# Where a Trainium2 kernel takes its norm roots, and in which order three engines meet between a gated layer and a linear attention

## The chip, the cores and the metric

One core of one Trainium2 chip. The metric is the time of the kernel on the device in microseconds, the median of several runs. Five engines of the core work side by side, each through its own list of instructions, and wait for each other on semaphores: TensorE (PE, with its weight loads as PEld), VectorE (DVE), ScalarE (ACT), GpSimd (POOL) and SyncE (SP), which issues the DMAs.

## What is computed

Four sequences (B = 4) of 512 rows by 256 columns, float32, go through four parts, with a residual and a normalisation over the columns after each:

```
x = layernorm(x + attention_0(x))      # softmax attention
x = layernorm(x + wave(x))             # gated layer, below
x = layernorm(x + attention_1(x))      # linear attention
x = layernorm(x + mlp(x))              # six blocks, 256 -> 1024 -> 256

wave: h = (cos(ph) + sin(ph)) * amp                # amp = sigmoid, ph = tanh of x @ weights
      for l in range(2):
          h = layernorm(h + (h @ ent_w[l]) @ ent_pw[l])
          h = layernorm(h + sum over two paths of h @ path_w[l] * mod[l])
attention_1: q = elu(x Wq)+1, k = elu(x Wk)+1, v = x Wv
      out = (q (k^T v)) / (q . sum(k)),  then @ Wo
```

The change touches the wave, attention_1 and the first turn of the MLP. What they compute stays the same.

## The kernel before

Every product is made from two parts of each float32 operand, a high part (rounded to the engine's format, ScalarE) and a low part (the remainder, VectorE), in three matmuls: high by high, high by low, low by high. So every tensor that goes into TensorE passes through ScalarE and then VectorE.

**The wave.** The two products of half a layer are folded into one 256x256 matrix, so the wave is four *stages* (STAGES = 4, END = 3) of one product and one normalisation for each of the four sequences b. One pass of one sequence is: `linear(st, b)` on TensorE into two PSUM banks (L1652, L1654); `moments(st, b)` on VectorE, that is mean and variance from PSUM (L2200, L2204); the *root*, one over the square root of the variance by an integer start value and two polynomial steps; `normalise(st, b)` on ScalarE (L1944), which needs the root's scale and shift; `turn` on TensorE, the transposes (L1661); `high` on ScalarE (L1951); `low` on VectorE (L2219); and then the next stage's `linear`. After the stages comes `sum_up(b)` on VectorE: the last gain, the residual (L2227, L2230), moments again; `output_of_wave(b)` on ScalarE (L1960) writes attention_1's input, `final_turn(b, c)` on TensorE (L1672) transposes it, `output_high` (L1955) and `output_low` (L2237) split it.

**Where a root is taken.** `ON_VECTOR` and `ON_GPSIMD` list the keys ("stage", st, b), ("sum", b) and ("next", b). For a key of `ON_GPSIMD`, VectorE's `statistics` stops after the moments and raises `v_mv`, and GpSimd's `root` takes 14 small dependent instructions (L135 to L146, L1604, L1606) and raises `g_scale`. For a key of `ON_VECTOR`, VectorE itself goes on with 9 steps (L96 to L121) and one for the shift (L2192), and raises `v_scale`. GpSimd takes its roots one by one in the order of the list.

**Attention_1.** For each b six *units* (`unit(b, at)`: four of keys and values, two of queries; TensorE L1699, ScalarE L1972, L1973, L1979, VectorE L2252), then `key_values` (L1713), `block_diagonal` (L2262), `numerators` in two halves (L1728), `divide` (L2271, L2273, L2278), `transpose_attention` (L1741), `attention_high` and `attention_low` (L1988, L2287), `project` (L1750), `residual_next` (L2294), `moments_next`, a root with the key ("next", b), `normalise_next` (L1997), `transpose_next` (L1762) and the halves `next_high` and `next_low` (L2003, L2303). TensorE may start unit n when ScalarE has done unit n - 3. Behind it come the MLP's `hidden` (L1808), `gelu` (L2049, L2050) and `gelu_low` (L2326), and `output` (L1825).

**What sets the order.** The order on each engine is written out by hand, as a list of such calls; an engine that waits holds up everything behind it in its own list. Two waits outside these lists matter here. SyncE loads the MLP's rows over the memory of the wave's sums once the last `output_of_wave` is done:

```
sp.wait_ge(wave["a_norm"], number("sum", B - 1))
for tile, name in ((g.mlp_b2, ...), (g.mlp_g, ...), (g.mlp_b, ...)):
    sp.dma_start(tile, ...).then_inc(rows_in, 16)
```

and GpSimd waits for these rows before the first root of a "next" key, since it adds them right behind (L1616 to x_a, L1621 to mlp_b):

```
pool.wait_ge(rows_in, 16 * 4)
for b in range(B):
    if b < B - 1:
        root("next", b)
```

## Time and profile before

| What | us |
|---|---|
| median of 3 runs (1121.85 to 1127.71) | 1122.81 |
| the profiled execution: its own time | 1125.32 |
| the profiled execution: span of the trace | 1123.6 |
| TensorE busy | 1020.4 (91%) |
| VectorE busy | 749.5 (67%) |
| ScalarE busy | 621.6 (55%) |
| GpSimd busy | 355.9 (32%) |
| chain that ended last: PE, DVE, ACT, POOL | 71%, 13%, 6%, 4% |

Attention_0 and the start of the wave's gates take the first 353 us of the span, the wave's stages run to about 441, attention_1 with the first pieces of the MLP to 563, and the MLP to the end. The share of an engine is an average over all of these; what a change in one stretch is worth has to be read in that stretch.

### The profile page before, as it was taken

The page shows a single profiled execution, that of the slowest core. Times are in us where ns is not written, and L with a number is a line of the kernel's source. Part 1 is how long each engine was busy: PE and PEld are TensorE (multiplying, and loading weights), DVE is VectorE, ACT ScalarE, POOL GpSimd, SP SyncE. Part 2 cuts the span into 40 slices and gives each one's busy share as a digit, 9 for nine tenths or more (in the row PEclk, how much of TensorE's full clock was granted, in tenths as well). Part 3 has the DMA queues.
Part 4 walks back from the last instruction along what each step waited for, and adds up shares of the span by engine and source line. Part 5 has one row for each costly group of instructions (what it writes and reads, how often), then busy time and mean ns, then how long its engine had stood idle before and what let it go on. Part 6 is the DMA issues. An engine that isn't in the chain of part 4 may idle for free.

```text
span 1123.6 us, 18216 instructions
## 1 busy us (share of the span) xinstructions
PE 1020.4 (91%) x6589; PEld 847.2 (75%) x6589; DVE 749.5 (67%) x2023; ACT 621.6 (55%) x1200; POOL 355.9 (32%) x704
## 2 busy tenths in 40 slices
PE   6788998989988787878799999999999999999996
PEld 5455555555656686666698999988999899998896
DVE  4676775867628567757656776666776777666756
ACT  4466565664358455645565664566645666456650
POOL 3454354461122555413201224212232122321500
PEclk9599988998989899789999999999999999999998
DMA  7000000022110001011110110101011011010111
GB/s 234 20 2 20 2 20 20 21 58 76 57 43 3 1 1 38 1 75 57 39 57 1 38 31 9 38 1 38 2 38 38 1 38 38 1 38 1 38 39 38
DMA packets 29234, 36.91 MB, mean 33 GB/s; under 512 B 1780, under 2 KB 26584, under 8 KB 29144
## 3 DMA queue, kind: packets, MB, share of 16 engines
q1 hardware_dynamic: 24600, 31.02, 8.5%
q10 hardware_dynamic: 4544, 4.72, 1.4%
q8 instruction: 53, 0.87, 0.3%
q14 instruction: 37, 0.30, 0.1%
HBM read 31.40 MB, written 4.20 MB: 32 GB/s over the span
## 4 chain that ended last, share of the span: by engine, by line
PE 71%; DVE 13%; ACT 6%; issue 4%; POOL 4%; DMA 1%; SPq 0%; DVEq 0%; ACTq 0%; POOLq 0%
PE ps L1825 23%; PE ps L1808 23%; PE ps L853 3%; PE ps L806 3%; PE ps L830 3%; DVE ps L1065 3%; PE ps L901 2%; PE ps L1781 2%; PE ps L860 2%; PE ps L1351 1%; PE ps L817 1%; DVE ln_stats L2200 1%; PE ps L1699 1%; PE ps L1652 1%; PE ps L869 1%
## 5 line engine op out<-in xcount | busy, mean ns | idle before, releaser
L2049 ACT ACTIVATE G<-ps,bias_col 128x512 f32<-128x512 f32 x192 | 135.4, 705 | 181.3 <-PE ps L1808 171.8
L1825 PE MATMUL ps<-w_h,G_h 128*128 128x256 f32 x736 | 208.2, 283 | 0.0
L1825 PE MATMUL ps<-w_h,G_l 128*128 128x256 f32 x736 | 207.9, 282 | 0.0
L1825 PE MATMUL ps<-w_l,G_h 128*128 128x256 f32 x736 | 207.8, 282 | 0.0
L2326 DVE TENSOR_TENSOR G_l<-G,G_h 128x512 fp32r<-128x512 f32 x192 | 155.1, 816 | 63.3 <-ACT G_h L2050 63.2
L1628 POOL TENSOR_TENSOR x_a<-xn,mlp_g 128x1024 f32<-128x1024 f32 x20 | 67.6, 3378 | 350.1 <-DVE xn L2356 350.1
L681 ACT ACTIVATE probs<-ps 128x512 f32<-128x512 f32 (+3 forms) x256 | 98.3, 440 | 113.1 <-PE ps L817 112.9
L1808 PE MATMUL ps<-xT_h,w_h 128*128 128x512 f32 x384 | 152.0, 396 | 1.6 <-ACT G_h L2050 1.6
L1065 DVE CUSTOM_DVE_ANT_0 ps<-ps,q_mask 128x128 f32<-128x128 f32 (+3 forms) x256 | 120.7, 512 | 46.8 <-PE ps L806 45.3
L1808 PE MATMUL ps<-xT_h,w_l 128*128 128x512 f32 x384 | 150.6, 392 | 0.0
L1808 PE MATMUL ps<-xT_l,w_h 128*128 128x512 f32 x384 | 150.3, 391 | 0.0
L1825 PEld LDWEIGHTS ps<-w_h,G_h 128*128 128x128 f32 x736 | 139.9, 190 | 0.7
L1825 PEld LDWEIGHTS ps<-w_h,G_l 128*128 128x128 f32 x736 | 140.3, 191 | 0.0
L1825 PEld LDWEIGHTS ps<-w_l,G_h 128*128 128x128 f32 x736 | 139.5, 190 | 0.8
L2050 ACT ACTIVATE G_h<-ps,bias_col 128x512 fp32r<-128x512 f32 x192 | 134.9, 703 | 0.0
L2340 DVE TENSOR_TENSOR rsum<-ps,x_a 128x1024 f32<-128x1024 f32 x23 | 28.2, 1225 | 105.2 <-PE ps L1825 105.2
L569 POOL TENSOR_SCALAR_AFFINE_SELECT probs<-probs 128x256 f32<-128x256 f32 x128 | 53.1, 416 | 123.4 <-ACT probs L681 123.4
L1808 PEld LDWEIGHTS ps<-xT_h,w_h 128*128 128x128 f32 x384 | 72.1, 188 | 16.8 <-ACT G_h L2050 2.1
L1808 PEld LDWEIGHTS ps<-xT_h,w_l 128*128 128x128 f32 x384 | 72.1, 188 | 15.6
L1808 PEld LDWEIGHTS ps<-xT_l,w_h 128*128 128x128 f32 x384 | 72.2, 188 | 15.0
L806 PE MATMUL ps<-heads_T 64*128 64x128 f32 (+3 forms) x256 | 73.2, 450 | 10.8 <-DVE top_score L1065 9.7
L2320 DVE TENSOR_TENSOR xT_l<-hs,xT_h 128x512 fp32r<-128x512 f32 x40 | 77.0, 1952 | 2.3 <-ACT xT_h L2035 1.1
(298 smaller groups left out, 2142.4 us busy)
## 6 DMA issues: line engine op xcount, KB each, us to landing
w_raw<-L_ffn_W_T SPq DMA_DIRECT2D x12, 1024.0 KB, 5.1
hs<-L_attn_hidden_states SPq DMA_DIRECT2D x8, 512.0 KB, 4.0
...
heads_T<-neg_rows SPq DMA_DIRECT2D x64, 2.0 KB
```

Source lines behind the costliest of these rows:

```text
L569: pool.affine_select(diagonal, diagonal, [[0, 2], [1, P]], ALU.is_ge, 0.0, base=0, channel_multiplier=-1).then_inc(s["g_sel"], 1)
L681: act.activation(probs[:, p % 2, o, OFF[j]:OFF[j] + COLS[j]], ps[:, score_bank(r, o), 0:COLS[j]], ACT.Exp).then_inc(s["a_exp"], 1)
L806: pe.matmul(ps[:, o, 0:(t + 1) * P], heads_T[rows, p // UP, 0, p % UP, t * P:(t + 1) * P], heads_T[rows, p // UP, 1, p % UP, 0:(t + 1) * P ...
L830: mm = pe.matmul(outputs[rows:rows + 2 * DH, j * P:S], val[:, j, 4 * q + h, :], probs[:, h // 2, h % 2, OFF[j]:OFF[j] + COLS[j]], start=(r ...
L1065: v.tensor_tensor_reduce(ps[:, o, 0:(t + 1) * P], ps[:, o, 0:(t + 1) * P], q_mask[:, S - (t + 1) * P:S], 1.0, MASKED, ALU.add, ALU.max, to ...
L1628: pool.tensor_tensor(g.x_a[:, rows, :], xn[:, b % 2, :, :], bcast(g.mlp_g[:, i, :], 1, [P, RT, D]), ALU.mult).then_inc(feed["g_mul"], 1)
L1808: mm = pe.matmul(ps[:, hidden_bank(i, n), :], w[:, c, f * P:(f + 1) * P], x[:, b, c, :], start=(k == 0), stop=(k == 5))
L1825: mm = pe.matmul(ps[:, 4 + t // 2, (t % 2) * D:(t % 2 + 1) * D], x[b % 2][f][:, t * P:(t + 1) * P], w2_chunk(w, f), start=(k == 0), stop=( ...
L2049: act.activation(G32[n % 4], bank, ACT.Gelu, bias=bias)
L2050: act.activation(G_h[b % 2][f], bank, ACT.Gelu, bias=bias).then_inc(feed["a_g"], 1)
L2320: v.tensor_tensor(g.xT_l[:, b, c, :], src, g.xT_h[:, b, c, :].bitcast(F32), ALU.subtract).then_inc(feed["v_T"], 1)
L2326: v.tensor_tensor(G_l[b % 2][f], G32[n % 4], G_h[b % 2][f].bitcast(F32), ALU.subtract).then_inc(feed["v_gl"], 1)
```

## The change

1. Three roots go from GpSimd to VectorE: ("stage", 0, 0), ("stage", END, 0) and ("next", 2). `moments` becomes a generator, and `gated_low(2)` is put between the moments and the steps of the first of these roots.
2. On ScalarE at the wave's begin, `gated_high(2)` goes ahead of the sines of b = 3, and `normalise(0, 2)` goes behind `high(0, 0)`.
3. At the wave's end, VectorE's first two instructions of `sum_up(0)` go ahead of the last `low`, and the rest right behind it.
4. In attention_1, `block_diagonal(0)` goes ahead of the end of `sum_up(2)`, whose statistics go behind `unit(1, 0)`; `divide(0, 1)` goes ahead of the start of `sum_up(3)`; the two final turns of b = 3 go behind unit(2, 2) and unit(2, 4) (TensorE, and their halves on ScalarE and VectorE); `output_of_wave(3)` on ScalarE goes behind unit(2, 0).
5. At the MLP's begin, the first two `hidden` go ahead of `key_values(3)` and of the second `transpose_next` of b = 1, with a wait of `hidden` for its own bank alone, and `gelu`, `gelu_low`, `attention_high(3)` and `attention_low(3)` are moved to fit.

```diff
...
     NORMS = [("stage", st, b) for st in range(STAGES) for b in range(B) if (st, b) < (END, 2)]
     NORMS += [("sum", 0), ("stage", END, 2), ("sum", 1), ("stage", END, 3), ("sum", 2), ("sum", 3)]
     NORMS += [("next", b) for b in range(B)]
-    ON_VECTOR = [("sum", 0), ("sum", 1), ("next", B - 1)]
-    ON_GPSIMD = [("stage", st, b) for st in range(STAGES) for b in range(B)]
-    ON_GPSIMD += [("sum", 2), ("sum", 3), *(("next", b) for b in range(B - 1))]
+    ON_VECTOR = [("stage", 0, 0), ("stage", END, 0), ("sum", 0), ("sum", 1), ("next", 2), ("next", 3)]
+    ON_GPSIMD = [key for key in NORMS if key not in ON_VECTOR]
...
-        for key in ON_GPSIMD[:1 - B]:
-            root(*key)
+        for key in ON_GPSIMD:
+            if key[0] != "next":
+                root(*key)
         pool.wait_ge(rows_in, 16 * 4)
         for b in range(B):
-            if b < B - 1:
+            if ("next", b) in ON_GPSIMD:
                 root("next", b)
...
                 if b == 0 and f % 2 == 0 and not early:
                     pe.wait_ge(feed["v_w"], i * 8 - 4 + f // 2 + 1)
                 if early and n < 3:
-                    pe.wait_ge(second["a_exp"], B * UNITS)
+
+                    pe.wait_ge(second["a_exp"], B * UNITS - 2 + n)
                     pe.wait_ge(second["a_v"], B * RT)
                 elif early and n in (*range(3, FC), FC + 1, FC + 2):
                     pe.wait_ge(feed["a_g"], n - 2)
...
         unit(1, 5)
         key_values(1)
         project(0)
-        final_turn(3, 0)
         numerators(1, 0)
         unit(2, 0)
-        final_turn(3, 1)
         numerators(1, 1)
         unit(2, 1)
         transpose_attention(1)
-        for at in range(2, UNITS):
-            unit(2, at)
+        unit(2, 2)
+        final_turn(3, 0)
+        unit(2, 3)
+        unit(2, 4)
+        final_turn(3, 1)
+        unit(2, 5)
         key_values(2)
         project(1)
         transpose_next(0, 0)
...
         transpose_attention(2)
         for at in range(2, UNITS):
             unit(3, at)
+        hidden(0, 0, (0,))
         key_values(3)
         project(2)
         transpose_next(1, 0)
         numerators(3, 0)
+        hidden(0, 0, (1,))
         transpose_next(1, 1)
-        hidden(0, 0, (0, 1))
         numerators(3, 1)
         hidden(0, 0, (2, 3))
         transpose_attention(3)
...
         gated_high(act, g, 1)
         for n in range(4 * (B - 1), 4 * B):
             gate_function(act, g, n)
+        gated_high(act, g, 2)
         half_angle(act, g, 3)
-        gated_high(act, g, 2)
         whole_angle(act, g, 3)
         normalise(0, 0)
         gated_high(act, g, 3)
         normalise(0, 1)
-        normalise(0, 2)
         for st in range(END):
 
             for b in range(B):
                 high(st, b)
-                if (st, b) != (0, 0):
-                    normalise(*divmod(st * B + b + 2, B))
+                normalise(*divmod(st * B + b + 2, B))
...
         output_high(2, 1)
         unit(1, 4)
         unit(1, 5)
+        unit(2, 0)
         output_of_wave(3)
-        output_high(3, 0)
-        unit(2, 0)
-        output_high(3, 1)
         unit(2, 1)
         attention_high(1)
         unit(2, 2)
+        output_high(3, 0)
+        unit(2, 3)
         normalise_next(0)
-        for at in range(3, UNITS):
-            unit(2, at)
+        unit(2, 4)
+        output_high(3, 1)
+        unit(2, 5)
...
         normalise_next(1)
         for at in range(3, UNITS):
             unit(3, at)
+        gelu(0, 0, 0)
         next_high(1, 0)
+        gelu(0, 0, 1)
         next_high(1, 1)
-        gelu(0, 0, 0)
-        gelu(0, 0, 1)
         normalise_next(2)
         gelu(0, 0, 2)
+        attention_high(3)
         gelu(0, 0, 3)
-        attention_high(3)
         gelu(0, 0, 4)
         gelu(0, 0, 5)
         next_high(2, 0)
...
             if st + b == 0:
 
                 v.wait_ge(first["g_x1"], B + 1)
-            for _ in statistics(banks(b), ("stage", st, b)):
-                pass
+            yield from statistics(banks(b), ("stage", st, b))
 
         def low(st, b):
             for c in range(KC):
...
                 low_next(i, 0)
 
 
+        def run(steps, count=100):
+            for _ in range(count):
+                next(steps, None)
+
         square(v, g, chain, 1)
         gated_low(v, g, 0)
         gated(v, g, chain, 1)
         square(v, g, chain, 2)
         gated_low(v, g, 1)
         gated(v, g, chain, 2)
-        moments(0, 0)
+        steps = moments(0, 0)
+        run(steps, 2)
         gated_low(v, g, 2)
+        run(steps)
         square(v, g, chain, 3)
         gated(v, g, chain, 3)
-        moments(0, 1)
+        run(moments(0, 1))
         gated_low(v, g, 3)
-        moments(0, 2)
+        run(moments(0, 2))
         for st in range(END):
             if st == 1:
                 v.wait_ge(wave["a_l1"], 3)
...
             for b, (later, done) in TURN:
-                low(st, b)
-                if (st, b) != (END - 1, B - 1):
-                    moments(st + later, done)
-
-        def run(steps, count=100):
-            for _ in range(count):
-                next(steps, None)
-
-        run(sum_up(0))
-        moments(END, 2)
+                if (st, b) == (END - 1, B - 1):
+
+                    steps = sum_up(0)
+                    run(steps, 2)
+                    low(st, b)
+                    run(steps)
+                    run(moments(END, 2))
+                else:
+                    low(st, b)
+                    run(moments(st + later, done))
+
         steps = sum_up(1)
         run(steps, 1)
         for c in range(KC):
...
         unit(0, 1)
         run(steps)
         unit(0, 2)
-        moments(END, 3)
+        run(moments(END, 3))
         unit(0, 3)
         steps = sum_up(2)
         run(steps, 1)
...
         for c in range(KC):
             output_low(1, c)
         unit(0, 5)
+        block_diagonal(0)
+        run(steps, 1)
+        unit(1, 0)
         run(steps)
-        block_diagonal(0)
-        unit(1, 0)
         divide(0, 0)
         unit(1, 1)
+        divide(0, 1)
         steps = sum_up(3)
         run(steps, 1)
-        divide(0, 1)
         unit(1, 2)
         output_low(2, 0)
         unit(1, 3)
...
         run(steps)
         unit(1, 5)
         block_diagonal(1)
-        output_low(3, 0)
+        residual_next(0)
         divide(1, 0)
         unit(2, 0)
-        residual_next(0)
-        output_low(3, 1)
         run(moments_next(0))
         divide(1, 1)
         unit(2, 1)
         attention_low(1)
-        for at in range(2, UNITS):
-            unit(2, at)
+        unit(2, 2)
+        output_low(3, 0)
+        unit(2, 3)
+        output_low(3, 1)
+        unit(2, 4)
+        unit(2, 5)
...
         for at in range(2, UNITS):
             unit(3, at)
         block_diagonal(3)
+        gelu_low(0, 0, 0)
         residual_next(2)
         next_low(1, 0)
         divide(3, 0)
         run(moments_next(2))
+        gelu_low(0, 0, 1)
         next_low(1, 1)
-        gelu_low(0, 0, 0)
         divide(3, 1)
-        gelu_low(0, 0, 1)
         gelu_low(0, 0, 2)
+        attention_low(3)
         gelu_low(0, 0, 3)
-        attention_low(3)
         gelu_low(0, 0, 4)
         gelu_low(0, 0, 5)
         residual_next(3)
```

**The first place is VectorE at the wave's begin**, from the last gate of b = 2 on (`amp` is what the gate gives, `x_b` its work tile, L1396 is `gated_low`). Before:

```order
L1385 SCALAR_TENSOR_TENSOR amp<-x_b,amp 128x1024
L2200 BN_STATS ln_stats<-ps 128x6 x4
L2204 BN_AGGR norm_mv<-ln_stats 128x2 x4
L1396 TENSOR_TENSOR xT_l<-amp,xT_h 128x1024
L1375 SCALAR_TENSOR_TENSOR x_b<-x_b 128x1024
```

and now:

```order
L1385 SCALAR_TENSOR_TENSOR amp<-x_b,amp 128x1024
L86 BN_STATS ln_stats<-ps 128x6 x4
L91 BN_AGGR ln_mv<-ln_stats 128x2 x4
L1396 TENSOR_TENSOR xT_l<-amp,xT_h 128x1024
L96 TENSOR_SCALAR ln_var<-ln_mv 128x4
L99 TENSOR_SCALAR norm_factors<-ln_var 128x4
L103 TENSOR_TENSOR ln_t<-norm_factors 128x4
...
L121 SCALAR_TENSOR_TENSOR norm_factors<-ln_t,norm_factors 128x4
L2195 SCALAR_TENSOR_TENSOR norm_factors<-ln_mv,norm_factors 128x4
L1375 SCALAR_TENSOR_TENSOR x_b<-x_b 128x1024
```

The root's ten small instructions stand between `gated_low(2)` and the square of b = 3.

On ScalarE at the same place, before and then now (L1365 and L1370 are the sines of b = 3, L1391 `gated_high`, L1944 and L1948 `normalise`, L1951 and L1955 `high`):

```order
L1365 ACT_TABLE_LOAD
L1365 ACTIVATE x_b<-tanh 128x1024
L1391 ACTIVATE xT_h<-amp 128x1024
L1370 ACTIVATE tanh<-tanh 128x1024
L1944 ACTIVATE xn<-ps,norm_shift,norm_scale 128x256 x4
L1391 ACTIVATE xT_h<-amp 128x1024
L1944 ACTIVATE xn<-ps,norm_shift,norm_scale 128x256 x4
L1944 ACTIVATE hs<-ps,norm_shift,norm_scale 128x256 x4
L1951 ACTIVATE xT_h<-ps 128x512 x4
```

```order
L1391 ACTIVATE xT_h<-amp 128x1024
L1365 ACT_TABLE_LOAD
L1365 ACTIVATE x_b<-tanh 128x1024
L1370 ACTIVATE tanh<-tanh 128x1024
L1948 ACTIVATE xn<-ps,norm_factors 128x256 x4
L1391 ACTIVATE xT_h<-amp 128x1024
L1948 ACTIVATE xn<-ps,norm_shift,norm_scale 128x256 x4
L1955 ACTIVATE xT_h<-ps 128x512 x2
L1948 ACTIVATE hs<-ps,norm_shift,norm_scale 128x256 x4
```

The first `high` no longer stands behind the third `normalise`.

**The second place is VectorE at the wave's end** (L2227 and L2229 are the first instruction of `sum_up`, the last L2219 or L2221 is the last `low`). Before:

```order
L2204 BN_AGGR norm_mv<-ln_stats 128x2 x4
L2219 TENSOR_TENSOR xT_l<-ps,xT_h 128x512 x2
L2227 TENSOR_TENSOR amp<-xn,last_g 128x1024
L2230 TENSOR_TENSOR amp<-amp,x_a 128x1024
L86 BN_STATS ln_stats<-amp 128x6 x4
```

and now:

```order
L2207 BN_AGGR norm_mv<-ln_stats 128x2 x4
L2229 TENSOR_TENSOR amp<-xn,last_g 128x1024
L2232 TENSOR_TENSOR amp<-amp,x_a 128x1024
L2221 TENSOR_TENSOR xT_l<-ps,xT_h 128x512 x2
L86 BN_STATS ln_stats<-amp 128x6 x4
```

The sum's two long instructions stand ahead of the last low part.

**The third place is VectorE around the third of the residuals of attention_1** (rsum; G_l_0 and G_l_1 are the low parts of the first two gelu tiles, z and att the divisions of b = 3). Before:

```order
L2294 TENSOR_TENSOR rsum<-ps,x_b 128x1024
L2303 TENSOR_TENSOR xT_l<-ps,xT_h 128x512
L2271 TENSOR_SCALAR z<-ps 128x32
L2273 RECIPROCAL z<-z 128x32
L2278 TENSOR_TENSOR att_5532<-ps,z 128x256 x2
L2200 BN_STATS ln_stats<-rsum 128x6 x4
L2204 BN_AGGR norm_mv<-ln_stats 128x2 x4
L2303 TENSOR_TENSOR xT_l<-ps,xT_h 128x512
L2326 TENSOR_TENSOR G_l_0_5560<-G_0_5576,G_h_0_5544 128x512
L2271 TENSOR_SCALAR z<-ps 128x32
```

and now:

```order
L2328 TENSOR_TENSOR G_l_0_5560<-G_0_5576,G_h_0_5544 128x512
L2296 TENSOR_TENSOR rsum<-ps,x_b 128x1024
L2305 TENSOR_TENSOR xT_l<-ps,xT_h 128x512
...
L86 BN_STATS ln_stats<-rsum 128x6 x4
L91 BN_AGGR ln_mv<-ln_stats 128x2 x4
L96 TENSOR_SCALAR ln_var<-ln_mv 128x4
...
L2195 SCALAR_TENSOR_TENSOR norm_factors<-ln_mv,norm_factors 128x4
L2328 TENSOR_TENSOR G_l_1_5561<-G_1_5577,G_h_1_5545 128x512
L2305 TENSOR_TENSOR xT_l<-ps,xT_h 128x512
L2273 TENSOR_SCALAR z<-ps 128x32
```

The steps of the root now stand ahead of the second division of b = 3.

## Rows read from the trace of the kernel before

**Rows 1.** Busy time by stretch; PE, PEld, DVE, ACT, POOL busy, then granted clock, DMA share, GB/s.
```profile
353.00:383.00 30.00, 18.17 (x131) 16.72 (x129) 19.02 (x37) 18.48 (x27) 13.31 (x43) 0.93 0.01 3
...
563.00:1100.00 537.00, 537.00 (x3491) 490.56 (x3490) 367.63 (x777) 308.77 (x504) 134.36 (x45) 1.00 0.08 25
```
**Rows 2.** Timeline, ScalarE, wave's begin; start, us, engine, line, operation [idle before <-releaser].
```profile
370.32 1.94 ACT L1944 ACTIVATE xn<-ps,norm_shift,norm_scale 128x256 f32<-128x256 f32 x4 [5.29 <-POOL norm_shift L1606]
...
375.73 1.94 ACT L1944 ACTIVATE xn<-ps,norm_shift,norm_scale 128x256 f32<-128x256 f32 x4 [2.53 <-POOL norm_shift L1606]
...
382.15 2.07 ACT L1951 ACTIVATE xT_h<-ps 128x512 fp32r<-128x512 f32 x4
```
**Rows 3.** Timeline, first and last of the 14 instructions of one GpSimd root.
```profile
418.25 0.19 POOL L135 TENSOR_SCALAR norm_var<-norm_mv 128x4 f32<-128x4 f32 x1 [0.60 <-POOL norm_shift L1606]
...
421.94 0.23 POOL L1606 TENSOR_SCALAR norm_shift<-norm_shift 128x4 f32<-128x4 f32 x1
```
**Rows 4.** Timeline, VectorE, the wave's last two passes and the first sum.
```profile
434.87 1.29 DVE L2219 TENSOR_TENSOR xT_l<-ps,xT_h 128x512 fp32r<-128x512 f32 x2 [1.59 <-ACT xT_h L1951]
436.08 1.41 DVE L2200 BATCH_NORM_STATS2 ln_stats<-ps 128x6 f32<-128x256 f32 x4
...
439.83 1.29 DVE L2219 TENSOR_TENSOR xT_l<-ps,xT_h 128x512 fp32r<-128x512 f32 x2 [1.92 <-ACT xT_h L1951]
441.04 1.21 DVE L2227 TENSOR_TENSOR amp<-xn,last_g 128x1024 f32<-128x1024 f32 x1
...
445.40 0.17 DVE L96 TENSOR_SCALAR ln_var<-ln_mv 128x4 f32<-128x4 f32 x1
...
447.18 0.16 DVE L2192 SCALAR_TENSOR_TENSOR norm_factors<-ln_mv,norm_factors 128x4 f32<-128x4 f32 x1
```
**Rows 5.** Timeline, ScalarE, the first output of the wave.
```profile
447.38 2.07 ACT L1960 ACTIVATE x_b<-amp,norm_factors 128x256 f32<-128x256 f32 x4 [1.52 <-DVE norm_factors L2192]
```
**Rows 6.** Timeline, VectorE's third gated low part.
```profile
364.11 1.23 DVE L1396 TENSOR_TENSOR xT_l<-amp,xT_h 128x1024 fp32r<-128x1024 f32 x1 [1.69 <-ACT xT_h L1391]
```
**Rows 7.** Timeline, GpSimd in the same microsecond, in the root of ("stage", 0, 0).
```profile
364.20 1.20 POOL L141 TENSOR_TENSOR norm_t<-norm_scale 128x4 f32<-128x4 f32 x1
```
**Rows 8.** Busy time of PE by stretch, with the granted clock, ahead of the first final turn.
```profile
446.00:448.00 2.00, 0.00 (x0) 0.84 0.00 0
```
**Rows 9.** Timeline, ScalarE, the last stage's normalise of b = 3.
```profile
469.41 1.94 ACT L1944 ACTIVATE hs<-ps,norm_shift,norm_scale 128x256 f32<-128x256 f32 x4 [2.90 <-POOL norm_shift L1606]
```
**Rows 10.** Timeline, VectorE, unit(1, 0).
```profile
471.93 0.42 DVE L2252 SCALAR_TENSOR_TENSOR k<-ex,pos 128x256 f32<-128x256 f32 x1 [1.14 <-ACT pos L1973]
```
**Rows 11.** Timeline, GpSimd's start on the roots of ("sum", 2) and ("next", 0), then mlp_b.
```profile
470.54 0.19 POOL L135 TENSOR_SCALAR norm_var<-norm_mv 128x4 f32<-128x4 f32 x1 [1.17 <-issue]
...
503.66 0.20 POOL L135 TENSOR_SCALAR norm_var<-norm_mv 128x4 f32<-128x4 f32 x1 [12.38 <-DVE norm_mv L2204]
...
514.08 3.11 POOL L1621 TENSOR_TENSOR mlp_b<-mlp_b,mlp_b 128x1280 f32<-128x1280 f32 x1
```
**Rows 12.** Timeline, ScalarE, output_of_wave(3) and normalise_next(0).
```profile
491.31 2.07 ACT L1960 ACTIVATE x_b<-amp,norm_shift,norm_scale 128x256 f32<-128x256 f32 x4 [6.04 <-POOL norm_shift L1606]
...
509.53 2.08 ACT L1997 ACTIVATE hs<-rsum,norm_shift,norm_scale 128x256 f32<-128x256 f32 x4
```
**Rows 13.** The last of the rows' DMAs: its issue by SyncE.
```profile
494.26 0.43 SPq L1543 DMA_DIRECT2D mlp_b<-L_ffn_LN_B  x1
```
**Rows 14.** The same DMA: size and median us from issue to landing.
```profile
mlp_b<-L_ffn_LN_B SPq DMA_DIRECT2D x1, 640.0 KB, 6.1
```
**Rows 15.** Timeline, TensorE, the first numerators of b = 2.
```profile
521.08 1.19 PE L1728 MATMUL ps<-bd,q 128*128 128x136 f32 x8 [1.38 <-DVE bd L2263]
```
**Rows 16.** Timeline, VectorE, the moments of ("next", 2).
```profile
544.99 1.39 DVE L2200 BATCH_NORM_STATS2 ln_stats<-rsum 128x6 f32<-128x256 f32 x4
```
**Rows 17.** Timeline, ScalarE, normalise_next(2).
```profile
551.65 2.08 ACT L1997 ACTIVATE hs<-rsum,norm_shift,norm_scale 128x256 f32<-128x256 f32 x4 [2.69 <-POOL norm_shift L1606]
```
**Rows 18.** The chain that ended last, in order of time: the last projection.
```profile
558.65 4.38 PE ps L1750 x24
```

## Prediction

> **What bounds the kernel now.** I read the busy time by stretch first, to see where the end can be moved. From 563 us on TensorE is busy for all 537 of 537 us at full clock, while between 353 and 383 it is busy for 18.2 of 30 [rows 1]. So before 563 the kernel waits, behind it the MLP takes what it takes, and a microsecond won in front of 563 moves the end by a microsecond. Then I read the timelines of the four engines from 353 to 563 side by side, with the waits in brackets, and asked at each idle stretch of TensorE which call came last. Three places answer for what the change touches.
>
> At the wave's begin ScalarE waits 5.29 us for the first root and 2.53 for the second, and reaches the first `high` at 382.15, behind three normalises [rows 2]. In the stages a pass is a loop of two slots: normalise 1.94 [rows 2], half a `high` (0.5), `low` 1.29 and moments 1.8 [rows 4], a GpSimd root from 418.25 to 422.17, that is 3.92 [rows 3], some 0.1 between each. Together 9.7 for two passes; the last two `low` are 4.96 apart [rows 4]. At the end `output_of_wave(0)` starts at 447.38 and frees TensorE at 449.45 [rows 5]. In attention_1 TensorE waits for `output_of_wave(3)`, which itself waited 6.04 for its root [rows 12], and later for VectorE.
>
> The numbers below are replays: I take each engine's new list, give every call its duration from the rows, and start it at the latest of its waits and the end of the call ahead of it. All times are in the clock of the old trace.
>
> **The wave's begin.** `gated_high(2)` now comes right after the gates, so `gated_low(2)` runs in the gap behind the moments instead of waiting 1.69 until 364.11 [rows 6], and ends about 363.6. The ten small steps take 1.94, from 445.40 to 447.34 where VectorE does them today [rows 4], so the first scale is there at 365.6 and `normalise(0, 0)` starts then and not at 370.32 [rows 2]: 4.7 earlier. It doesn't help by itself. The second root still runs on GpSimd, and its moments are pushed behind the ten steps: they end at about 371.0 against 370.8. `normalise(0, 1)` starts near 376.0 instead of 375.73 [rows 2]. What counts is that the first `high` comes next, at 377.9 and not 382.15 [rows 2]. That is **4.3 us**.
>
> A port matters here. GpSimd's instruction at 364.20 took 1.20 [rows 7] where its like take 0.2, and ended with VectorE's 1024-column low part (364.11 to 365.34) [rows 6]. `gated_low(3)` now starts with the second root and costs it 1.0, which is in the sum. The Trainium skill (SBUF — State Buffer, "Who interferes with whom") states that VectorE with two SBUF inputs and GpSimd hold a shared port in turn, and whoever starts first keeps it for its whole instruction. By that rule the second root could lose 0 instead of 1.0 if GpSimd starts first; the rows here show the loss, the trace agrees with the lock, and the sum keeps 1.0.
>
> **The stages.** The loop is the same, so the 4.3 is carried, with one more saving. ("stage", END, 0) costs 1.94 on VectorE in place of 3.92 on GpSimd: 2.0. But ScalarE is then still in the normalise ahead of it and has a `high` to do first, so about 1.1 of it comes through for `normalise(END, 0)`, and the ten steps delay VectorE's next `low` little, which had 1.59 of slack [rows 4]. Also the second `high` ran right behind the first one and found its inputs late; now the even passes are up to 6 us earlier than before and the odd ones 4.5 to 5. The replay has `normalise(END, 0)` end at 432.5 (old 439.3) and the last moments of stage END, b = 1, end at 433.1.
>
> **The wave's end.** `sum_up(0)` waited for the last `low` until 441.04 [rows 4]. Now it starts at 433.1, its two long instructions (1.21 and 1.23) end at 435.6, and the last `low` follows, ending at 436.8, 4.3 ahead of the old 441.12. Statistics 1.8 and ten steps 1.94 end at 440.6. GpSimd's root of (END, 1) meets the long instructions as it does today and ends near 439.1, `normalise(END, 1)` takes ScalarE until 441.1, and then `output_of_wave(0)` goes at 441.1 instead of 447.38 [rows 5]. So the wave is **6.3 us** earlier. Bounds: 4.3, if nothing is won in or behind the stages, and 8.3, if the clock stays up as well. The clock: in 446 to 448, with TensorE idle, the granted clock is 0.84 of full, so it fell to 1.2 GHz at about 447.4 [rows 8], some 2.5 after the last product; the replay's new idle is 2.6. I count nothing for it and keep 2 us for the upper end.
>
> **Attention_1, middle.** Here is the trap. Measured in a clock shifted by the 6.3, `block_diagonal(0)` no longer waits behind sum 2, which frees the first numerators by 2.5. But sum 2's statistics now stand behind unit(1, 0), which waits for ScalarE's normalise of 469.41 [rows 9] and runs at 471.93 to 472.35 [rows 10]. With 1.8 of statistics GpSimd starts that root at 474.2, not 470.54 [rows 11]; its output leaves ScalarE 2.4 later, and so does what follows, up to project(0), ending at 491.1. There the moved final turn pays: numerators(1, 0) and unit(2, 0) no longer wait for `output_of_wave(3)`, and run 3 to 4 us earlier than before. But ScalarE now does unit(2, 0) first, so `output_of_wave(3)` ends near 496.6 and not 493.38 [rows 12]. The MLP's rows follow it: the last is issued at 494.26 [rows 13] and lands 6.1 later [rows 14], 7.0 behind the output. That is 503.6 now. GpSimd sits on this wait ahead of the root of ("next", 0), whose moments are ready at 496.5. So the root runs from 503.7, the same time as today's 503.66 [rows 11], and of the 5 to 6 us that TensorE had won almost all is given back. Only ScalarE is now free when the root is done: `normalise_next(0)` goes at 507.7 instead of 509.53 [rows 12]. The addition to mlp_b (3.11) [rows 11] blocks VectorE's queries as before, and the numerators of b = 2, at 521.08 today [rows 15], go at 519.3 to 519.6. **1.5 us**. TensorE idles some 7 us ahead of them; the products behind run at half clock, but VectorE's divisions are later than they. Bounds: -2 (the half clock and the later root both show) and +5 (the rows land in time).
>
> **The MLP's begin.** The first `hidden` fits into TensorE's wait ahead of key_values(3), and the second into the one ahead of the transposes, so numerators(3, 1) comes 1.7 earlier. The root of ("next", 2): moments start at 544.99 [rows 16], 1.8 and 1.94 later the factors are there, at 548.8, and `normalise_next(2)` starts at 548.85 instead of 551.65 [rows 17]: 2.8 earlier. VectorE pays with 1.94 ahead of the second division, which ends at 551.5 rather than 549.8, and the attention's transposes end at 552.5, 0.6 late. But the third gelu is done at 552.1 and `attention_high(3)` follows it directly. GpSimd's addition (551.1 to 553.5) holds one low part, then comes `attention_low(3)`, and the last project starts at 555.5 instead of 558.65 [rows 18]. **3.1 us**; its 4.38 [rows 18] is a run at half clock, and at full clock it would be 1.4 less. Bounds: 0.6 (VectorE's longer list cancels the root) and 4.5.
>
> **Sum.** 6.3 + 1.5 + 3.1 = 10.9. Against the profiled execution's 1125.32 that is 1114.4. The median of the three runs is 2.5 below that execution, at 1122.81; 10.9 below it is **1111.9**, my forecast. A measurement of this kernel tells about 0.5%, or 5.6 us, from no change.
>
> **The rivals.** (A) *The clock stays up* in the idle of the first final turn and at the last project: 2 and 1.4 more, 1108.5. For it: both idles shrink to about the length at which it fell. Against: rows of exactly that length show it falling. 0.22. (B) *The middle loses*: sum 2's late root and the late rows are dearer than I think, -2 instead of +1.5, and the tail gives 2: 6.3 - 2 + 2 = 6.3, 1116.5. For it: every wait there is on the edge and TensorE goes cold. 0.2. (C) *No change to be told*: the second root bounds the wave's begin, a cold TensorE in the first stages eats 2 of the 4.3, the middle gives -1 and the tail 0.6: 4.3 - 2 + 1 of the wave's end, -1, +0.6, so 2.9, 1119.9. 0.1. (D) *Slower*: `output_of_wave(3)` decides. Each microsecond by which it slips delays the rows, GpSimd's root, `normalise_next(0)` with units (2, 4) and (2, 5) queued behind it, and the numerators of b = 2. It loses from the point at which it ends 10.9 later than my 496.6, which eats the whole sum, that is when as much as another root (3.9) and another landing (7.0) come in between; at 15 later the kernel takes 1122.8 + 4.1 = 1126.9. The rows show GpSimd idle there, so 0.03. That the change doesn't do what it says is no case: the new lists are fixed.
>
> **How the numbers follow.** Forecast 0.45, A 0.22, B 0.2, C 0.1, D 0.03. The forecast's own range is 1109.5 to 1114.5. The range for eight in ten takes in A and most of B: 1107 to 1118. Faster by over 0.5% (below 1117.2) are the forecast, A and most of B: 0.85; same 0.12; slower 0.03.
>
> **What would show it.** First `high` about 4 us earlier on ScalarE, with one GpSimd root between it and normalise(0, 0); first final turn at 443; GpSimd's root of ("next", 0) starting with the landing of mlp_b, with a wait of some 7 us ahead of it, and TensorE idle ahead of numerators(2, 0); the last project at about 547.7. I am wrong if that root starts with its moments, if the first final turn is not 5 us or more earlier, or if the MLP from its first full turn on takes longer than today.

## The result, and the profile after

| | before | after |
|---|---|---|
| median, 4 runs of each | 1122.33 us (1115.84 to 1127.71) | **1107.94 us** (1106.56 to 1111.8) |
| profiled execution, own time | 1125.32 | 1107.9 |
| its span | 1123.6 | 1106.2 |

The ratio of the runs is estimated at 0.9884 with a 95% interval of 0.9836 to 0.9932: 1.16% or 13.0 us faster, where 10.9 were forecast; the two medians are 14.4 apart. The time is inside the range, 4.0 us below the forecast. Of those 4, 0.5 is the level of the runs: the forecast started from 1122.81.

The page of the changed kernel gives the shares. 13 us are hardly seen in them, since they were idle time.

```profile
span 1106.2 us, 18200 instructions
...
PE 1013.3 (92%) x6589; PEld 841.9 (76%) x6589; DVE 752.4 (68%) x2053; ACT 620.3 (56%) x1200; POOL 342.6 (31%) x662
```

**A marker for reading the two traces.** The spans differ by 17.4 us, which is more than the medians do. Where does that come from? I take as zero the start of the last gate instruction of b = 2 on VectorE (L1385), the last one whose predecessors the change leaves alone, and call it M. M is at 359.46 before and at 355.51 after. So 3.95 of the 17.4 lie in front of everything that was changed, and 13.4 behind it. All times "from M" below are free of the first part.

| us from M: start of | before | before, again | after | after, again |
|---|---|---|---|---|
| M itself, in the span | 359.46 | 357.09 | 355.51 | 356.89 |
| `normalise(0, 0)` | 10.9 | 10.9 | 6.0 | 6.0 |
| first `high` | 22.7 | 22.6 | 18.2 | 18.1 |
| `output_of_wave(0)` | 87.9 | 88.2 | 81.2 | 81.2 |
| `output_of_wave(1)` | 101.2 | 101.5 | 94.5 | 92.6 |
| `output_of_wave(3)` | 131.9 | 131.8 | 128.2 | 126.3 |
| GpSimd's root of ("next", 0) | 144.2 | 144.3 | 137.3 | 135.4 |
| `normalise_next(0)` | 150.1 | 149.4 | 141.3 | 139.3 |
| numerators(2, 0) | 161.6 | 161.0 | 152.4 | 150.5 |
| last `project` | 199.2 | 200.2 | 187.3 | 185.4 |
| end of the span | 764.1 | 765.2 | 750.7 | 748.7 |

**The wave's begin.** ScalarE's timeline after (start, us, engine, line, operation, idle before). `normalise(0, 0)` goes at 361.50 and the second root's wait is now the one of 5.57 us, in front of 371.85. The `high` at 373.66 follows at once, where before a third normalise lay between [rows 2].

```profile
361.50 1.93 ACT L1948 ACTIVATE xn<-ps,norm_factors 128x256 f32<-128x256 f32 x4 [0.20 <-DVE norm_factors L2195]
365.22 1.06 ACT L1391 ACTIVATE xT_h<-amp 128x1024 fp32r<-128x1024 f32 x1 [1.80 <-DVE amp L1385]
...
371.85 1.93 ACT L1948 ACTIVATE xn<-ps,norm_shift,norm_scale 128x256 f32<-128x256 f32 x4 [5.57 <-POOL norm_shift L1605]
373.66 1.09 ACT L1955 ACTIVATE xT_h<-ps 128x512 fp32r<-128x512 f32 x2
```

**The wave's end.** VectorE after: the two long instructions of the sum stand ahead of the last `low` and not behind it [rows 4].

```profile
428.89 1.19 DVE L2229 TENSOR_TENSOR amp<-xn,last_g 128x1024 f32<-128x1024 f32 x1
430.12 1.23 DVE L2232 TENSOR_TENSOR amp<-amp,x_a 128x1024 f32<-128x1024 f32 x1
431.26 1.28 DVE L2221 TENSOR_TENSOR xT_l<-ps,xT_h 128x512 fp32r<-128x512 f32 x2
...
434.31 0.17 DVE L96 TENSOR_SCALAR ln_var<-ln_mv 128x4 f32<-128x4 f32 x1
...
436.09 0.16 DVE L2195 SCALAR_TENSOR_TENSOR norm_factors<-ln_mv,norm_factors 128x4 f32<-128x4 f32 x1
```

ScalarE after (L1964 is `output_of_wave`, L2001 `normalise_next`). `output_of_wave(0)` at 436.69 has no wait any more [rows 5]: ScalarE itself is late, since the normalise ahead of it waited 5.91 for GpSimd. Below, `output_of_wave(3)` at 483.73 has no wait either, and `normalise_next(0)` and `normalise_next(2)` follow.

```profile
434.88 1.93 ACT L1948 ACTIVATE xn<-ps,norm_shift,norm_scale 128x256 f32<-128x256 f32 x4 [5.91 <-POOL norm_shift L1605]
436.69 2.08 ACT L1964 ACTIVATE x_b<-amp,norm_factors 128x256 f32<-128x256 f32 x4
...
483.73 2.07 ACT L1964 ACTIVATE x_b<-amp,norm_shift,norm_scale 128x256 f32<-128x256 f32 x4
...
496.78 2.08 ACT L2001 ACTIVATE hs<-rsum,norm_shift,norm_scale 128x256 f32<-128x256 f32 x4 [4.40 <-POOL norm_shift L1605]
...
536.49 2.07 ACT L2001 ACTIVATE hs<-rsum,norm_factors 128x256 f32<-128x256 f32 x4 [2.61 <-DVE norm_factors L2195]
```

**The middle.** GpSimd after: the root of ("next", 0) waits 9.71 us for a DMA, that of `mlp_b`, and not for its moments as before [rows 11]. `output_of_wave(3)` ended at 483.73 + 2.07 = 485.80, and the root starts 7.05 behind it. Of the 9.71, 2.75 would be there without the DMA (run 4). Then comes the addition to mlp_b.

```profile
492.85 0.19 POOL L135 TENSOR_SCALAR norm_var<-norm_mv 128x4 f32<-128x4 f32 x1 [9.71 <-DMA mlp_b<-L_ffn_LN_B]
...
499.00 2.35 POOL L1616 TENSOR_TENSOR x_a<-hs,mlp_b 128x1024 f32<-128x1024 f32 x1 [2.26 <-ACT hs L2001]
501.30 3.34 POOL L1621 TENSOR_TENSOR mlp_b<-mlp_b,mlp_b 128x1280 f32<-128x1280 f32 x1
```

The same DMA stands in the chain that ended last, after (start, us, what). Of it read how the chain goes from ScalarE's output into a DMA queue and back to a normalise, with TensorE nowhere in those 13 us. The last line is the last projection, 4.38 before [rows 18].

```profile
483.85 1.95 ACT x_b L1964 x4
486.20 0.43 SPq L1542
486.68 6.03 DMA mlp_b<-L_ffn_LN_B
...
497.28 1.57 ACT hs L2001 x3
...
542.85 3.00 PE ps L1750 x24
```

VectorE in the same place, then TensorE. The two `q` took 4.25 together beside GpSimd's 3.34 us instruction (one alone takes 0.68 or 0.69 elsewhere, and in the trace before one took 3.41 beside the same addition, of 3.11 there), and TensorE idled 6.13 ahead of numerators(2, 0), where it idled 1.38 before [rows 15].

```profile
500.33 0.69 DVE L2239 TENSOR_TENSOR xT_l<-ps,xT_h 128x512 fp32r<-128x512 f32 x1 [7.77 <-ACT xT_h L1959]
500.94 4.25 DVE L2254 SCALAR_TENSOR_TENSOR q<-ex,pos 128x512 f32<-128x512 f32 x2
505.11 2.35 DVE L2503 TENSOR_TENSOR w_l<-w_raw,w_h 128x1024 fp32r<-128x1024 f32 x2
```

```profile
507.93 1.50 PE L1728 MATMUL ps<-bd,q 128*128 128x136 f32 x5 [6.13 <-DVE bd L2265]
```

### The profile page after: what moved, and what is told of

It reads as the page before. It is cut to its first block, busy times and chain, and to the rows that moved or that the text cites. A ratio compares the mean times of both kernels' runs of the same rounds, so it can differ in the third digit from the quotient of the medians.

```text
span 1106.2 us, 18200 instructions
## 1 busy us (share of the span) xinstructions
PE 1013.3 (92%) x6589; PEld 841.9 (76%) x6589; DVE 752.4 (68%) x2053; ACT 620.3 (56%) x1200; POOL 342.6 (31%) x662
## 4 chain that ended last, share of the span: by engine, by line
PE 51%; DVE 3%; ACT 1%; issue 1%; DMA 1%; POOL 0%; SPq 0%; DVEq 0%; ACTq 0%; POOLq 0%
PE ps L1826 24%; PE ps L1809 23%; PE ps L1781 2%; PE ps L1699 1%; DMA mlp_b<-L_ffn_LN_B 1%; PE ps L1750 1%; DVE ln_stats L86 0%; PE ps L1728 0%; ACT x_b L1964 0%; ACT hs L2001 0%; PE ps L1741 0%; DVE q L2254 0%; DVE w_l L2503 0%; DVE k L2254 0%; ACT pos L1977 0%
## 5 line engine op out<-in xcount | busy, mean ns | idle before, releaser
L1628 POOL TENSOR_TENSOR x_a<-xn,mlp_g 128x1024 f32<-128x1024 f32 x20 | 67.6, 3378 | 350.1 <-DVE xn L2358 350.1
```

The source lines that it names most:

```text
L1628: pool.tensor_tensor(g.x_a[:, rows, :], xn[:, b % 2, :, :], bcast(g.mlp_g[:, i, :], 1, [P, RT, D]), ALU.mult).then_inc(feed["g_mul"], 1)
```

## Experiments

Each kernel is the changed one with the edit shown, but for the first. A time without "median" is of one execution. Beside the first eight, kernels before ran at a median of 1120.8 (7 runs); beside the last four, on another chip, at 1125.05 (11 runs).

**1. The kernel before, once more.** No edit.

> The kernel before, unchanged, for a second trace of it. Times are read from M, the start of the last gate instruction of b = 2 on VectorE (359.46 us in the first trace of before, 355.51 in that of after); nothing ahead of M is changed. Theory 1, the 3.95 us between the two M is scatter from one execution to the next: M lies anywhere within some us of these two, while the distances from M repeat within 0.5: first high at M + 22.7, output_of_wave(0) at M + 87.9, numerators(2, 0) at M + 161.6, last project at M + 199.2, end of the span at M + 764. Theory 2, the change itself moves M: M is 359.5 again within 0.5.

1123.98 us. From M it repeats the first profile within 0.7 us up to numerators(2, 0) and within 1.1 behind them (table above), where 0.5 was expected. M itself moved by 2.4. So stretches behind M can be compared to about 1 us from single profiles, and whole times can't.

**2. ScalarE's old order at the wave's begin.**

```diff
-        gated_high(act, g, 2)
         half_angle(act, g, 3)
+        gated_high(act, g, 2)
...
         normalise(0, 1)
+        normalise(0, 2)
...
-                normalise(*divmod(st * B + b + 2, B))
+                if (st, b) != (0, 0):
+                    normalise(*divmod(st * B + b + 2, B))
```

> After, with ScalarE's order at the wave's begin as before (high(0, 0) behind the third normalise, gated_high(2) behind the first sine), and the root of (stage, 0, 0) still on VectorE. Theory 1, ScalarE's order brings the begin: the first high waits for the third root and normalise, so it starts at about M + 22 instead of M + 18.2, and output_of_wave(0) at about M + 85, 4 us later than in after. Theory 2, the root on VectorE brings it: the first high stays within 1 us of M + 18.2.

1114.23 us. ScalarE of this kernel: the first normalise still has its factors from VectorE, but three normalises stand ahead of the first `high`.

```profile
362.37 1.93 ACT L1948 ACTIVATE xn<-ps,norm_factors 128x256 f32<-128x256 f32 x4 [2.21 <-DVE norm_factors L2197]
...
376.73 1.94 ACT L1948 ACTIVATE hs<-ps,norm_shift,norm_scale 128x256 f32<-128x256 f32 x4 [2.06 <-POOL norm_shift L1605]
378.55 2.07 ACT L1955 ACTIVATE xT_h<-ps 128x512 fp32r<-128x512 f32 x4
```

The first `high` is at 378.55 - 354.59 (its M) = 24.0 from M, later than in the kernel before (22.7), and `output_of_wave(0)` at 88.2, the old place, where 85 was expected. **Without the order on ScalarE the whole gain of the wave is gone.** The roots on VectorE and the earlier sum are worth nothing there by themselves. The two moves were taken back together, and no run has the new order alone with everything else old.

**3. Root ("stage", 0, 0) back on GpSimd**, its key taken out of `ON_VECTOR`.

```diff
-    ON_VECTOR = [("stage", 0, 0), ("stage", END, 0), ("sum", 0), ("sum", 1), ("next", 2), ("next", 3)]
+    ON_VECTOR = [("stage", END, 0), ("sum", 0), ("sum", 1), ("next", 2), ("next", 3)]
```

> After, with the root of (stage, 0, 0) on GpSimd again and all else as in after, ScalarE's new order too. Theory 1, this root gives nothing by itself, since the second one on GpSimd decides: the first root ends about 4.5 us later than in after, but the first high starts at M + 18.2 to M + 18.8 and output_of_wave(0) within 0.7 us of M + 81.2. Theory 2, it is needed: the second root now queues behind the first on GpSimd (a contended one takes 7.8 us) and the first high is 2 us or more late.

1109.26 us. ScalarE of this kernel:

```profile
367.20 1.93 ACT L1948 ACTIVATE xn<-ps,norm_shift,norm_scale 128x256 f32<-128x256 f32 x4 [5.16 <-POOL norm_shift L1605]
372.02 1.93 ACT L1948 ACTIVATE xn<-ps,norm_shift,norm_scale 128x256 f32<-128x256 f32 x4 [1.94 <-POOL norm_shift L1605]
373.83 1.09 ACT L1955 ACTIVATE xT_h<-ps 128x512 fp32r<-128x512 f32 x2
```

`normalise(0, 0)` is 4.9 later (10.9 from M), yet the first `high` is 0.6 *earlier* (17.6), and `output_of_wave(0)` at 81.4 is the same as with the change (81.2). A root that comes 4.9 us sooner is worth nothing, because the next root gates the first `high`.

**4. GpSimd's wait for the MLP's rows behind the root of ("next", 0).**

```diff
-        pool.wait_ge(rows_in, 16 * 4)
         for b in range(B):
             if ("next", b) in ON_GPSIMD:
                 root("next", b)
+            if b == 0:
+                pool.wait_ge(rows_in, 16 * 4)
```

> After, with GpSimd's wait for the MLP's rows moved behind the root of (next, 0); the rows are only read by the additions behind it. Theory 1, that wait gives back what the moved final turns win: the root starts with its moments, some 7 us earlier than in after, normalise_next(0) some 4 us earlier (M + 137 instead of M + 141.3), numerators(2, 0) 3 to 4.4 us earlier than M + 152.4, and the kernel is 3 to 4 us faster than after. Theory 2, the additions on GpSimd and VectorE's queue behind them set the place: normalise_next(0) is earlier, but numerators(2, 0) within 1 us of M + 152.4, and so is the end.

Median 1105.88 us (4 runs), ratio to before 0.9881 (0.9815 to 0.9947), which times alone can't tell from the change's. GpSimd of this kernel:

```profile
486.38 0.19 POOL L135 TENSOR_SCALAR norm_var<-norm_mv 128x4 f32<-128x4 f32 x1 [2.75 <-issue]
...
494.99 2.38 POOL L1617 TENSOR_TENSOR x_a<-hs,mlp_b 128x1024 f32<-128x1024 f32 x1 [4.51 <-ACT hs L2002]
```

The root starts 2.75 us behind what GpSimd did last, and not 9.71. numerators(2, 0) come at 149.1 from M (152.4 with the change), the end at 746.6 (750.7). `output_of_wave(1)` is itself 0.6 later here (95.1), and from there numerators(2, 0) take 54.0 and not 57.9. So the rows did hold the middle, at a price of 3.9. The addition of `mlp_b`, 3.41 here, still costs VectorE its time.

**5. Root ("stage", END, 0) back on GpSimd**, by the same kind of edit.

```diff
-    ON_VECTOR = [("stage", 0, 0), ("stage", END, 0), ("sum", 0), ("sum", 1), ("next", 2), ("next", 3)]
+    ON_VECTOR = [("stage", 0, 0), ("sum", 0), ("sum", 1), ("next", 2), ("next", 3)]
```

> After, with the root of (stage, END, 0) on GpSimd again. Theory 1 (the replay), about half of the 2.0 us that it saves comes through: the GpSimd root would end 2 us later than VectorE's steps did, the sum starts 1.2 later, and output_of_wave(0) goes at M + 82 to M + 82.5 instead of M + 81.2; the end moves by the same 0.8 to 1.2. Theory 2, VectorE's ten steps cost its own queue as much as the root gains: output_of_wave(0) within 0.3 of M + 81.2.

1107.69 us. `output_of_wave(0)` at 82.2 from M, 1.0 later, and it waits for its root again:

```profile
436.76 2.07 ACT L1964 ACTIVATE x_b<-amp,norm_factors 128x256 f32<-128x256 f32 x4 [1.17 <-DVE norm_factors L2195]
```

The place alone would show nothing, since runs 4, 8 and 11, which have this part of the changed kernel as it is, stand at 82.3 to 82.4. But those are late already at the last normalise ahead of stage END (68.5 to 68.6 from M, 67.7 with the change), and this run isn't (67.6). From that normalise to `output_of_wave(0)` it takes 14.6 here and 13.5 to 13.8 in the five others read. So this root is worth 0.8 to 1.1, and the wave keeps 5.6 or more of its 6.7 without it. The end is at 751.4, 0.7 later.

**6. Root ("next", 2) back on GpSimd**, the same way.

```diff
-    ON_VECTOR = [("stage", 0, 0), ("stage", END, 0), ("sum", 0), ("sum", 1), ("next", 2), ("next", 3)]
+    ON_VECTOR = [("stage", 0, 0), ("stage", END, 0), ("sum", 0), ("sum", 1), ("next", 3)]
```

> After, with the root of (next, 2) on GpSimd again and the new order around it kept. Theory 1, this root is most of the 2.7 us won between the numerators of b = 2 and the last project: normalise_next(2) starts 2.4 later (M + 183.4 instead of M + 181.0), the last project 1.5 to 2 later (M + 189.1 instead of M + 187.3), and if TensorE's clock falls in the longer idle, the end is 3 us or more later. Theory 2, the order of hidden, gelu and attention_high(3) won it: the last project stays within 0.7 of M + 187.3.

1111.97 us. From numerators(2, 0) to the last project it takes 190.4 - 153.1 = 37.3; with the change 34.9; before 37.6. The root is nearly the whole gain there, 2.4 of 2.7. The new order around it does bring numerators(3, 1) forward, with the root on GpSimd too (24.9 behind numerators(2, 0), 26.1 before), but little of it reaches the last project. From the last project to the end it takes 563.4, as with the change (also 563.4) and not as before (764.1 - 199.2 = 564.9): the project ran at full clock here too, though TensorE idled ahead of it. TensorE of this kernel:

```profile
543.66 0.50 PE L1809 MATMUL ps<-xT_h,w_h 128*128 128x512 f32 x1 [2.68 <-ACT G_h L2054]
```

**7. The first sum behind the last `low` again.**

```diff
-                    steps = sum_up(0)
-                    run(steps, 2)
                     low(st, b)
-                    run(steps)
+                    run(sum_up(0))
```

> After, with the last low ahead of the whole of sum_up(0) again. Theory 1, from the trace of after: VectorE is free at M + 73.4, both the sum's input (M + 72.5) and the last high (M + 73.5) are there, so the two orders fill the same stretch and output_of_wave(0) stays within 0.4 of M + 81.2; this part of the change gives nothing. Theory 2, the sum must go first: output_of_wave(0) 1.2 us or more later.

1116.67 us, which is misleading: M is at 363.1 and not 355.5. From M, `output_of_wave(0)` is 0.3 later and the end 1.1, about the scatter of run 1. The earlier sum gives at most 0.3 at its own place. The 7.6 us of M come from unchanged code; see the last section.

**8. Part 4 of the change undone** on TensorE, ScalarE and VectorE: the final turns of b = 3 ahead of the numerators of b = 1, `output_of_wave(3)` ahead of unit(2, 0), sum 2 ahead of `block_diagonal(0)`. TensorE's part:

```diff
         project(0)
+        final_turn(3, 0)
         numerators(1, 0)
         unit(2, 0)
+        final_turn(3, 1)
         numerators(1, 1)
...
-        unit(2, 2)
-        final_turn(3, 0)
-        unit(2, 3)
-        unit(2, 4)
-        final_turn(3, 1)
-        unit(2, 5)
+        for at in range(2, UNITS):
+            unit(2, at)
```

> After, with the whole middle of attention_1 (block_diagonal(0), the sums 2 and 3, output_of_wave(3) and the two final turns of b = 3) in the order of before. Theory 1, the middle won 1.5 to 2.5 us: output_of_wave(0) at M + 81.2, output_of_wave(3) at M + 125 instead of M + 128.2, numerators(2, 0) at M + 154 to M + 155 instead of M + 152.4, and the end 1.5 to 2.5 later. Theory 2, since the rows come 3 us earlier in this order, the middle gave nothing: numerators(2, 0) within 0.7 of M + 152.4.

1110.45 us. From `output_of_wave(1)` to numerators(2, 0) it takes 60.4, as before (60.4), against 57.9 with the change. The end is at 753.0, 2.3 later from M, but `output_of_wave(1)` is 0.6 later here already; from there to the end it takes 657.9 against 656.2. Part 4 is worth 2.5 at numerators(2, 0) and 1.7 at the end.

**9. The change, once more**, beside the next three. No edit.

> The changed kernel once more, for its time beside the kernel before and the next two on one chip, and for a second trace. Both theories expect the distances of its first trace from M (the start of the last gate instruction of b = 2) within 0.7 us: output_of_wave(0) M + 81.2, numerators(2, 0) M + 152.4 to M + 153.1, last project M + 187.3 to M + 188, end M + 750.7 to M + 751.4; M itself anywhere from 354 to 363; the time 12 to 14 us below the kernel before.

Median 1112.01 us (6 runs, 1106.6 to 1117.71) against 1125.05 (11 runs): ratio 0.9891 (0.9851 to 0.9932), again 13.0 us. The distances from M were expected within 0.7 and are, up to `output_of_wave(0)`; from `output_of_wave(1)` on all is 1.9 earlier. In this profile the first final turn ran at full clock. TensorE by stretch (busy, granted clock, DMA share, GB/s) and its first final turn, first in the changed kernel's first profile, then in this one:

```profile
436.00:438.00 2.00, 0.16 (x2) 1.00 0.00 0
438.00:440.00 2.00, 1.18 (x6) 0.72 0.00 0
440.00:442.00 2.00, 0.79 (x4) 0.50 0.00 0
...
438.82 1.97 PE L1672 MATMUL ps<-ident,x_b 128*128 128x128 f32 x8 [2.66 <-ACT x_b L1964]
```

```profile
436.00:438.00 2.00, 2.00 (x11) 0.53 0.00 0
438.00:440.00 2.00, 1.11 (x10) 1.00 0.00 0
440.00:442.00 2.00, 1.09 (x8) 1.00 0.00 0
...
434.01 0.39 PE L1652 MATMUL ps<-stage_w_h,xT_h 128*128 128x256 f32 x1 [1.74 <-DVE xT_l L2221]
...
440.23 1.09 PE L1672 MATMUL ps<-ident,x_b 128*128 128x128 f32 x8 [1.12 <-ACT x_b L1964]
```

0.50 is 1.2 GHz, 1.00 is 2.4 GHz. The same program met the final turn in two ways. In the first profile the last products of the stages (L1652) ran at full clock, TensorE then idled 2.66 us, and the clock fell as the final turn began. In this one it fell some 6 us sooner, in those last products, behind an idle of 1.74 us. They ended later, so that only 1.12 us of idle was left, and the clock was back at 2.4 GHz when the final turn came. The slow products themselves cost nothing, since ScalarE waits for GpSimd there: `output_of_wave(0)` is at 81.2 in both. Runs 11 and 12 went the second way too (idle 1.12 and 1.14, full clock), and all seven profiles with an idle of 2.64 to 2.68 the first. The difference is worth 94.5 - 92.6 = 1.9 us, and all of it arrives at the end (750.7 against 748.7). Why the clock falls in one execution at the one place and in another at the other is open.

**10. The rows' wait late and the addition of mlp_b late**, the edits of run 4 and run 11 together; the one of run 11 is shown.

```diff
-            if b == 0:
-
-                pool.tensor_tensor(g.mlp_b[:, :, :], g.mlp_b[:, :, :], g.mlp_b2[:, 1:BLOCKS, :], ALU.add
-                                   ).then_inc(feed["g_bb"], 1)
+        pool.tensor_tensor(g.mlp_b[:, :, :], g.mlp_b[:, :, :], g.mlp_b2[:, 1:BLOCKS, :], ALU.add
+                           ).then_inc(feed["g_bb"], 1)
```

> After, with GpSimd's wait for the rows behind the root of (next, 0), and the addition to mlp_b behind all four additions to x_a. Theory 1, behind the rows it is the addition to mlp_b (3.1 to 3.3 us) that holds VectorE's last query and the weights' low parts: numerators(2, 0) go at M + 146 instead of M + 149.1, and the kernel is 5 to 7 us faster than after. Theory 2, ScalarE's weights and the final turn's low part come last there: numerators(2, 0) stay at M + 148.5 or later, and the gain is that of the rows alone, 4 us. What the late addition costs in the first MLP turn is open; up to 3 us if it holds a low part that TensorE needs.

**Median 1103.12 us** (6 runs, 1100.08 to 1106.73), ratio 0.9821 (0.9784 to 0.9858): 8.9 us below the change's median on the same chip and 21.9 below before. The two ratios' intervals still touch, but from `output_of_wave(1)` to the end it takes 649.5 where both profiles of the change take 656.2, so 6.7 of the 8.9 is seen in the trace. The best version of this study. VectorE of this kernel, and TensorE behind it:

```profile
494.52 0.69 DVE L2238 TENSOR_TENSOR xT_l<-ps,xT_h 128x512 fp32r<-128x512 f32 x1 [3.26 <-ACT xT_h L1958]
495.13 1.59 DVE L2253 SCALAR_TENSOR_TENSOR q<-ex,pos 128x512 f32<-128x512 f32 x2
```

```profile
499.46 1.19 PE L1727 MATMUL ps<-bd,q 128*128 128x136 f32 x8 [1.18 <-DVE bd L2264]
```

The two `q` took 1.59 and not 4.25, and TensorE idled 1.18 and not 6.13. From `output_of_wave(1)` to numerators(2, 0): 50.8 against 57.9. The end from M is at 743.9 against 750.7 and 748.7.

**11. The addition of mlp_b late alone**, the edit of run 10 without that of run 4.

> After, with the addition to mlp_b behind all four additions to x_a, and the rows' wait as in after. Theory 1 (the port), VectorE's last query of b = 2 and the low weights no longer wait for it: numerators(2, 0) 2.5 to 3.3 us earlier, at M + 149.5 to M + 150. Theory 2, VectorE is only late by its own list: within 0.7 of M + 152.7.

1106.3 us. The same stretch takes 55.3, so 2.6 less than 57.9; with the rows' 3.9 (54.0) that makes 6.5, and both together gave 7.1. The two faults add up. 1.4 is lost again behind (36.3 from there to the last project, 34.9 with the change), and from `output_of_wave(1)` to the end it takes 654.9, 1.3 less than with the change.

**12. The moved turns alone undone**: the final turns of b = 3, their halves, `output_of_wave(3)` and `residual_next(0)` in the old order; `block_diagonal(0)` ahead of sum 2 and the late sums stay. TensorE's part is that of run 8, and VectorE's is this:

```diff
         block_diagonal(1)
-        residual_next(0)
+        output_low(3, 0)
         divide(1, 0)
         unit(2, 0)
+        residual_next(0)
+        output_low(3, 1)
...
```

> After, with only the final turns of b = 3, their halves and output_of_wave(3) in the order of before; block_diagonal(0) and the sums 2 and 3 as in after. Theory 1, the moved turns carry the middle: TensorE waits for output_of_wave(3) again, about 5 us, numerators(1, 0) go at M + 130 to M + 131 instead of M + 124.9, and numerators(2, 0) at M + 156 to M + 157.5, later than with the whole middle old (M + 155.5), since sum 3 is later in this order. Theory 2, the early block_diagonal(0) carries it: numerators(2, 0) at M + 153 to M + 154.

1113.61 us. TensorE waits 4.74 for `output_of_wave(3)` again. The stretch takes 62.7, more than before (60.4). Hence inside part 4 the moved turns bring 4.8 (62.7 - 57.9), and the rest of it, block_diagonal(0) early and the sums late, costs 2.3 (62.7 - 60.4): `output_of_wave(2)` comes 17.8 behind `output_of_wave(1)` here and 15.2 in run 8. From M, numerators(2, 0) are at 155.2 and not at 156 or later as expected, since the first final turn ran at full clock in this profile.

## Why the prediction was right, and where it was small

**The wave's begin: right.** 4.3 was claimed at the first `high`, 4.5 came (22.7 to 18.2 from M). It was claimed that the root of (0, 0) doesn't help by itself and that ScalarE's order counts. Runs 2 and 3 show just that: `output_of_wave(0)` is 7.0 later without the order, more than the 6.7 that the change won there, and 0.2 later without the root. Runs that remove one part need not add up, and 2 shows why: with the old order the root on VectorE pushes the second moments back (they end 13.2 behind M, 11.4 before) and makes the first `high` later than before.

**The stages and the wave's end: right to 0.4.** Claimed 6.3 at `output_of_wave(0)`, measured 87.9 - 81.2 = 6.7 (7.0 against the repeat). Root ("stage", END, 0) was put at 1.1 and is worth 0.8 to 1.1 (run 5). The replay's new idle of TensorE was 2.6; it was 2.66 in the first profile and 1.12 in the second. In the replay the two slots of a stage add up to 9.45, and five gaps of 0.1 make 9.9 of it and not 9.7, which is what twice the 4.96 says; the forecast doesn't use it.

**The middle: the mechanism right, the size low by up to 1.** Put into the old clock by the wave's 6.7, `output_of_wave(3)` is 128.2 + 6.7 - 131.9 = 3.0 later; 3.2 was claimed. The rows land 7.05 behind its end (7.0). GpSimd's root then stands at 137.3 + 6.7 = 144.0, where it stood at 144.2 before: "the same time as today's". `normalise_next(0)` gained 2.1 (1.8 claimed), TensorE idled 6.1 ("some 7"), and 1.6 to 2.5 came through at numerators(2, 0) (57.9 against 59.5 and 60.4), where 1.5 was taken. Runs 4, 10 and 11 tell that both things the working named, the landing and the addition, were the limits. Their price at numerators(2, 0), counted from `output_of_wave(1)`: 3.9 for the one and 2.6 for the other.

**The MLP's begin: 2.7 for 3.1, nearly all from the root.** From numerators(2, 0) to the last project it took 37.6 and takes 34.9 in both profiles. (In the repeat of before it took 39.2, with the granted clock at 0.64 and 0.51 in the four microseconds from 534, that is at key_values(3) and the start of project(2).) Run 6 gives the root 2.4 of the 2.7. Of the 1.7 that the earlier `hidden` was to bring at numerators(3, 1), 1.2 came there and 0.3 at the last project.

**The mis-sized term: the clock at the last project.** The sum said of it that "at full clock it would be 1.4 less" and counted 0 in the forecast's 10.9. It took 4.38 before and 3.00 after. Nor was all of the 4.38 at half clock, as the prediction had it: it starts at 558.65, and the stretch up to 560 is still at 1.00. TensorE before, by stretch, then after:

```profile
558.00:560.00 2.00, 1.35 (x11) 1.00 0.00 0
560.00:562.00 2.00, 2.00 (x12) 0.50 0.00 0
562.00:564.00 2.00, 2.00 (x11) 0.65 0.00 0
```

```profile
542.00:544.00 2.00, 2.00 (x14) 1.00 0.00 0
544.00:546.00 2.00, 2.00 (x20) 1.00 0.00 0
```

From the start of that project to the end it took 564.9 and 565.0 in the two profiles of before, and 563.2 to 563.5 in the twelve profiles of the change and its variants. That it fell to 1.2 GHz before goes with the idle times ahead of it: 1.63, then 2.07 (L1808's and L1750's waits). But run 6 had 2.68 and 1.47 there and stayed at 2.4 GHz, so which idle decides is not settled.

The sum in measured terms: 6.7 + 2.5 + 2.7 + 1.5 = 13.4, the 13.4 behind M and close to the runs' 13.0. It is one pair of profiles; the second pair gives 765.2 - 748.7 = 16.5, and of these 3.1 more, 1.9 is the clock of the first final turn and 1.1 the later end of the repeat of before. Against 10.9 the terms were off by +0.4, +1.0, -0.4 and +1.5. So it is half of rival A that came true: its 1.4 at the last project in every profile of the change and its variants, its 2 at the first final turn in three of these twelve, and there because the clock had fallen sooner and was back. None of the three signs of being wrong showed: the root started with the landing, the first final turn was 6.7 earlier, and the MLP from the last project on was shorter. B, C and D did not happen. B's reason was sound (the landing and a cold TensorE are there), but it took its loss to be larger than what the moved turns bring, and they bring 4.8.
